# Attention and gated FFN on one core: a tile's scores are made one slot ahead of the slot in which VectorE takes them

## What is computed

```
Q, K, V = x @ W.T + b           # 16 heads of 16
scores = Q @ K.T / 4            # 512 x 512 per head
thresh = 31st largest of a row
scores = where(scores < thresh, -inf, scores)
context = softmax(scores) @ V
x = layernorm(x + context @ Wo.T + bo)
h = silu(x @ wg.T) * (x @ wu.T)
x = layernorm(x + h @ wd.T)
```

## Time and profile before

| | |
|---|---|
| median of 3 runs | 3061.3 us (3058.01 to 3065.76) |
| the profiled execution | 3046.8 us |
| its span | 3045.0 us |
| its mean granted TensorE clock | 0.951 |
| instructions | 81353 |

### The profile page before, as it was taken

One profiled execution on the slowest core, in us unless ns is written; L12 is line 12 of the kernel. 1 busy time (PEld: TensorE's weight loads), 2 busy tenths in 40 slices (PEclk: granted clock), 3 DMA queues, 4 the chain that ended last, 5 costly groups with the idle time before them and its releaser, 6 DMA issues.

```text
span 3045.0 us, 81353 instructions
## 1 busy us (share of the span) xinstructions
PE 2680.3 (88%) x21045; PEld 1454.1 (48%) x21375; DVE 2481.3 (81%) x12298; ACT 2480.9 (81%) x5894; POOL 2407.2 (79%) x1677
## 2 busy tenths in 40 slices
PE   5889989989998988889989999988989898899985
PEld 2444544545454444444545454444545454454443
DVE  4888888888888878888888888878888888888831
ACT  3788889888888977798888889978879887888931
POOL 1787988888888877788888889877869887888861
PEclk7889999999999999999999999999999999999976
DMA  2211111020111101011020111102011110202000
GB/s 81 48 25 38 28 39 39 25 47 26 41 25 40 39 22 43 18 41 39 25 46 25 43 23 44 36 25 46 26 36 30 34 43 19 47 20 50 2 15 7
DMA packets 91147, 102.67 MB, mean 34 GB/s; under 512 B 34514, under 2 KB 52947, under 8 KB 90579
## 3 DMA queue, kind: packets, MB, share of 16 engines
q1 hardware_dynamic: 88544, 93.73, 12.9%
q10 hardware_dynamic: 2034, 2.76, 0.3%
HBM read 20.86 MB, written 8.39 MB: 10 GB/s over the span
## 4 chain that ended last, share of the span: by engine, by line
PE 36%; DVE 19%; issue 14%; SPq 11%; POOL 10%; ACT 6%; DMA 2%; DVEq 1%; ACTq 0%; POOLq 0%
POOL mask L1070 8%; DVE cand L843 7%; PE bench L679 6%; SPq L349 6%; SPq L348 5%; PE Y_ps L608 5%; PE bench L673 4%; PE ST_ps L623 3%; DVE S L836 3%; PE Y_ps L606 3%; PE ctxT_ps L637 3%; PE bench L549 3%; PE ST_ps L620 2%; PE Y_ps L605 2%; ACT above L467 2%
## 5 line engine op out<-in xcount | busy, mean ns | idle before, releaser
L1070 POOL TENSOR_SCALAR mask<-S,thr,mb 128x512 bf16<-128x512 f32 x1024 | 2119.6, 2083 | 44.1 <-POOL mb L1064 30.0
L843 DVE MAX8 cand<-Y_ps 128x8 f32<-128x128 f32 x4096 | 1072.5, 282 | 5.3 <-issue 5.3
L457 ACT ACTIVATE junk<-S,at_zero,slope 128x512 bf16<-128x512 f32 x1024 | 824.6, 805 | 89.6 <-DVE S L836 89.5
L836 DVE TENSOR_SCALAR_CACHE_REDUCE S<-S_ps,na 128x512 f32<-128x512 f32 x1024 | 756.0, 738 | 163.2 <-PE S_ps L595 145.8
L467 ACT ACTIVATE above<-S,s,steep 128x512 bf16<-128x512 f32 x1024 | 824.5, 805 | 0.6
L475 ACT ACTIVATE PT<-ST_ps 128x512 f32<-128x512 f32 x1024 | 596.7, 583 | 205.7 <-PE ST_ps L623 200.2
L595 PE MATMUL S_ps<-KS,QS 64*128 64x512 f32 x1024 | 520.3, 508 | 4.2 <-DVE S L836 3.6
L608 PE MATMUL Y_ps<-KS,QS 64*128 64x512 f32 x1024 | 520.2, 508 | 0.0
L606 PE MATMUL Y_ps<-above,nbig 128*128 128x512 bf16 x1024 | 398.3, 389 | 85.4 <-DVE cand L843 57.4
L620 PE MATMUL ST_ps<-QS,KS 64*128 64x512 f32 x1024 | 415.4, 406 | 6.2 <-POOL mask L1070 6.2
L623 PEld LDWEIGHTS ST_ps<-nbig,mask 128*128 128x128 bf16 x4096 | 236.7, 99 | 382.5 <-issue 382.5
(11 more groups left out here) (125 smaller groups left out, 3682.1 us busy)
## 6 DMA issues: line engine op xcount, KB each, us to landing
QS<-Qhi SPq DMA_DIRECT2D x512, 32.0 KB, 2.0
KS<-Khi SPq DMA_DIRECT2D x512, 32.0 KB, 2.0
KS<-Klo SPq DMA_DIRECT2D x512, 32.0 KB, 2.0
QS<-Qlo SPq DMA_DIRECT2D x512, 32.0 KB, 2.0
xTs<-in_xT SPq DMA_DIRECT2D x17, 512.0 KB, 3.7
xs<-in_x SPq DMA_DIRECT2D x16, 512.0 KB, 3.9
out<-xs SPq DMA_DIRECT2D x16, 512.0 KB, 3.0
hT<-in_wgT ACTq DMA_DIRECT2D x1, 768.0 KB
```

The lines of the kernel that those rows point to most:

```text
L457: nc.scalar.activation(junk[:, :], S[:, score_place(j)[0], :], ACT.Tanh, bias=at_zero[:, :], scale=slope[:, hb, col:col + 1], accum_out=s0 ...
L836: nc.vector.tensor_scalar(S[:, at, :], S_ps[n % 2][:, :], na[:, hb, col:col + 1], None, ALU.add, op1=ALU.max, accum_out=rmax[:, n % RING:n ...
L843: mx = nc.vector.max(cand[:, j % CANDS, i, :], Y_ps[j % 2][:, i * BW:(i + 1) * BW])
L1070: nc.gpsimd.tensor_scalar(mask[:, h % MASKS, t, :], S[:, score_place(j)[0], :], thr[:, r:r + 1], mb[:, r:r + 1], ALU.is_lt, op1=ALU.add).t ...
```

## The change

TensorE's slot n now makes the scores of tile n+1 instead of those of tile n. Tile 0's scores are made ahead of slot 0 of batch 0, and slot 63 of a batch makes those of tile 0 of the next batch, except in the last batch, which for this reason stands outside the loop. The loop on TensorE therefore runs over batches 1 to 14, seven per turn. `scores` itself is unchanged but for a blank line (all later lines move by one): called for tile T+1 it waits until tile T-1 is evacuated. The other engines' programs are unchanged.

```
-TURN_OF, ACT_TURN_OF = 5, 7
+TURN_OF, ACT_TURN_OF, PE_TURN_OF = 5, 7, 7
...
-            def slots(b, first, rest):
+            def slots(b, first, rest, last=False):
                 for n in range(TILES):
                     T = b * TILES + n
                     if due(BELOW, n, first, rest):
                         below(T, n, first)
-                    if not rest:
-                        scores(T, n, b, first)
+                    if not rest and n + 1 < TILES:
+                        scores(T + 1, n + 1, b, first)
+                    if not rest and n + 1 == TILES and not last:
+                        scores(T + 1, 0, b + 1, False)
                     if due(TURNED, n, first, rest):
                         turned(T, n, first)
...
+            scores(0, 0, 0, True)
             slots(0, True, False)
...
-            with pe.Fori(1, B, TURN_OF) as b:
-                for i in range(TURN_OF):
+            with pe.Fori(1, B - 1, PE_TURN_OF) as b:
+                for i in range(PE_TURN_OF):
                     slots(b + i, False, False)
+            slots(B - 1, False, False, True)
             slots(B, False, True)
```

## The result

The changed kernel takes 3119.75 us (median of 4 runs, 3111.07 to 3124.09) against 3061.69 us before (4 runs); the ratio is 1.019 (95% interval 1.017 to 1.021), that is 52 to 63 us slower. Forecast were 3106 us and +45. The profiled execution of after has a span of 3122.3 us. It lies high among its runs and that of before low, so the two profiles differ by 77 us where the medians differ by 58.

What follows compares the result with a forecast made beforehand. No engine leads: TensorE is busiest and takes turns with VectorE. Waits and steps sum to 3.0 us a batch, +45 us over 15 batches on the 3061.3 us median: 3106 us, range 3076 to 3131 (8 in 10: 3050 to 3145).

Steps and rivals of the forecast that it cites:

- Slot 59: Scores wait for late evacuation 58, with TensorE's full down stretch right behind: +1.8 us a batch, bounds 0 and 1.8.
- slot 63: Turned scores 0.33 us later, VectorE's evacuation 0.46 us earlier: nothing, bounds -0.5 and +0.3 us.
- slots 0 to 10: Waits of 0.1 us each, 0.33 us in slots 3 and 7: nothing if TensorE's idle time stays, 1 us if not.
- 31 to 41: Steps in slots 35 and 39, with TensorE waiting around the transposes of 38 and 39: nothing, up to 0.6 us.
- Slot 11: VectorE's normalisation delays evacuation 10, so scores wait with the query projection behind them: +0.6 us, bounds 0.3 and 0.6.
- Slots 42 to 56: Three steps of 0.33 us in slots 43, 47, 51, less 0.43 us idle time: +0.6 us, bounds 0.2 and 1.0.
- The step: In 16 slots a batch (n mod 4 = 3) scores share a half with the below product and queue: 0.33 us each.
- Slots 14 to 31: Steps and late evacuations covered by SyncE's stacking copies and the load of xT: nothing, up to 1.3 us.
- The gains: VectorE's waits only move; a full stretch returns at most one evacuation, 0.75 us, at its end; none counted beyond slot 63.
- the lead pays: Rival: VectorE and ScalarE one evacuation ahead at ends of full stretches: -2.3 us a batch, 3027 us, chance 0.12.
- The loop: TensorE's body of seven batches instead of five, last batch behind it, one jump back instead of two: nothing.
- The marks named beforehand: Signs in the new profile: VectorE's score wait gone, TensorE's evacuation wait 30 us or more; wrong if maxima waits below 100.

Runs made afterwards that it cites:

- Experiments 2: Kernel before, no lead, scores in their own slot but waiting for the evacuation of tile T-1: ratio 1.019 to the kernel before, +58 us.
- 5: Changed kernel, but scores of tiles 59 and 60 made in their own slots: ratio 1.005 to the kernel before, +14 us.
- 6: Kernel before with the lead for tile 60 alone, its scores made in slot 59: ratio 1.016 to the kernel before, +50 us.
- experiment 10: Changed kernel with three filler copies of product L621 before the scores in slot 59, batches 1 to 15: ratio 1.014 to the kernel before, +43 us.
- experiment 7: Kernel before with the first turned product (L620) issued twice in slots with n mod 4 = 3: ratio 1.002 to the kernel before, +7 us.
- experiment 12: Changed kernel with the lead for tiles 0 to 8 only, other tiles in their own slot: ratio 1.0015 to the kernel before, +5 us.
- experiment 1: Kernel before with the loop part alone, seven batches per turn and batch 15 behind the loop, no lead: ratio 0.999 to the kernel before.
- experiment 4: Changed kernel with VectorE evacuating right behind the block maxima, ahead of bench work and moments: ratio 1.004 to the kernel before, +13 us.
- experiment 3: Kernel before with the score product issued twice in slots with n mod 4 = 3: ratio 1.001 to the kernel before.

## Why the prediction was right, step by step

**Slot 59 was the largest term, and is.** Forecast +1.8 us for the wait. Measured: 4.07 us before in 13 of 14 batches (5.29 in one, with a clock of 0.75), 5.77 us where the clock held, so +1.70. The assumed 0.15 us from the evacuation to the scores was 0.06. Experiments 2, 5 and 6 show that the cause is this wait, and above all in this place: the wait in every slot, without the lead, gives the whole loss (+58), the wait in slot 59 alone +50, and the change without it wins 44 of 58 us back.

**The step that failed is what stands behind it.** In 9 of 14 batches the slot took 7.35 to 7.44 us, 1.65 us on top, and in one 9.04, because the clock fell to half behind the idle time. The average is +2.9 instead of +1.8, 16 us in 15 batches, and experiment 10 wins 15 us by shortening the idle time from 1.20 to 0.50 us and not the wait. The length of the idle time alone does not decide it: before the change TensorE was idle 1.1 to 1.4 us ahead of the same slot in every batch (1.38 in the earlier trace rows), and the clock fell in one of 14; in the change the idle 1.20 us is the same in the four batches in which the clock held. What tips it is open.

**How near the number came is in part luck.** Forecast were 3.0 us a batch, the traces show 4.5. Slot 59 has 1.1 of the missing 1.5. The other errors below run from -1.0 to +1.2 us and only happen to leave 0.4 or 0.5. Against the medians 13 us are missing, against the two profiles 32.

**A slip in the range.** Its lower end takes 0.5 us for slot 59, where the walk through the batch gives 0, and leaves out slot 63 (-0.5); its upper end leaves out the bounds of slots 0 to 10 (1.0), 31 to 41 (0.6) and 63 (0.3). From the walk's own bounds it would have been wider, 3061 to 3160.

**Slot 11**, forecast +0.6: +0.55, and +0.13 in slot 13. Right to 0.1 us.

**Slots 42 to 56**, forecast +0.6: +0.3 up to slot 54. The step was mis-sized. In slot 51 and 52 of the change, batch 8:

```profile
1641.40 0.49 PE L609 MATMUL Y_ps<-KS,QS 64*128 64x512 f32 x1
1641.74 0.39 PE L596 MATMUL S_ps<-KS,QS 64*128 64x512 f32 x1
1641.97 0.39 PE L621 MATMUL ST_ps<-QS,KS 64*128 64x512 f32 x1
...
1644.06 0.50 PE L609 MATMUL Y_ps<-KS,QS 64*128 64x512 f32 x1
1644.07 0.49 PE L596 MATMUL S_ps<-KS,QS 64*128 64x512 f32 x1
1644.40 0.39 PE L621 MATMUL ST_ps<-QS,KS 64*128 64x512 f32 x1
```

In the slot with the shared half the scores do start 0.34 us behind, but the third product only 0.23 us behind them, so L621 comes 0.57 us after L609 where a normal slot has 0.34: the step is 0.23. Slots 51, 55 and 63 grow by 0.20 to 0.23. The Trainium skill's figure for a product of 512 columns, about 216 ns ("TensorE: Matmul & The Clock Gate", Back-to-back issue gap), was the better one here, and the row that I preferred shows the step behind the first product of a half; the one behind it is shorter. By experiment 7 all these steps together cost 7 us of the 58.

The cover was misread too. The 0.43 us of idle time that the forecast took off is not there: it is five gaps of 0.07 to 0.16 us at places where the trace of before lacks the record of L605. What covers instead does not show as idle time. In slot 43 of batch 8, before and after:

```profile
1586.22 0.40 PE L623 MATMUL ST_ps<-nbig,mask 128*128 128x128 bf16 x4
1586.59 1.20 PE L673 MATMUL bench<-x1T,wu 128*128 128x512 f32 x4
...
1620.41 0.40 PE L624 MATMUL ST_ps<-nbig,mask 128*128 128x128 bf16 x4
1620.61 1.18 PE L674 MATMUL bench<-x1T,wu 128*128 128x512 f32 x4
```

The bench product started 0.37 us behind the first mask product before and 0.20 behind it after. So 0.17 of the step of 0.23 us goes into a slack ahead of the bench product; it is so in slots 43 and 47 of every batch, which grow by 0.04 to 0.06 us. Slot 51 has no such slack and pays 0.21.

**Slots 14 to 31**, forecast nothing: +0.9 us. The load of xT, which was to cover, ends the wait of the projection only 3 times instead of 9. Slots 16 and 21 add 0.2 and 0.3. Slots 24 and 25 add 1.4, of which 23 and 26 give 0.9 back: the scores start 1.94 us late (2.0 forecast), and with the clock at half behind them (L621 of slot 24 takes 0.62 us in batch 8) the cover is not enough. The bound of 1.3 us held.

**The gains.** Slots 0 to 8 did win 1.0 us and 55 to 58 0.6 us, more than I allowed. But ScalarE was last behind the first: in slot 9 of batch 8 TensorE waits until ScalarE has copied the flags out of the bench (L446), which a ScalarE without a gap delivers no earlier. The copy of the context (L490) was done 0.63 us before the product started; behind it stood an exponentiation and then the flags.

```profile
1526.90 0.66 PE L647 MATMUL bench<-ident,ctxr 128*128 128x128 f32 x4 [1.27 <-ACT flag_i L446]
```

```profile
1524.87 0.83 ACT L457 ACTIVATE junk<-S,at_zero,slope 128x512 bf16<-128x512 f32 x1
...
1525.67 0.60 ACT L490 ACTIVATE ctxr<-ctxT_ps 128x512 f32<-128x512 f32 x1
1526.14 0.60 ACT L475 ACTIVATE PT<-ST_ps 128x512 f32<-128x512 f32 x1
1526.62 0.15 ACT L446 ACTIVATE flag_i<-bench 1x9 int32<-1x9 f32 x1
```

Over the span TensorE's product of slot 9 (L647) waits 16 times for this copy, 18.0 us in all; before the change it was six times and 1.9 us. In experiment 12 it is 16 times and 18.4 us.

That ScalarE and not VectorE is what ends last there is the point from which the rival "the lead pays" would have decided, and experiment 12 shows it alone. The win before slot 59 is lost in slot 59.

**The loop**: nothing, as forecast (experiment 1).

**The marks named beforehand**: VectorE's wait for scores gone, and TensorE's wait for evacuations above 30 us: seen. Slots 59 and 24 have 33 of the 38 us of it in batches 1 to 14, slot 11 under 1. In each slot with n mod 4 = 3 the scores start 0.33 us or more behind the below product: seen. TensorE's busy time can't be judged, for the missing records. TensorE's wait for maxima fell from 163 to 59 us, which I had called a sign of being wrong. It was not one, since the kernel got slower all the same: of the 104 us, 52 came back as waits for evacuations and 16 as waits for the flags in slot 9. The rest I put down to TensorE working longer, at the lower clock or on the added steps, which no run shows.

No version beat the kernel before. The one I would try next is experiment 4 with the lead taken out where it only adds the step; it was not run.

## What to carry to other kernels

Moving a producer one slot ahead with the same two buffers also moves its wait on the consumer one slot nearer, and everything queued behind it inherits that wait: before such a change, list for each slot when the consumer ends against when the producer starts, and look for the one slot in which lateness meets a full stretch. If the lead stays, the consumer should take the buffer first thing in its slot; that order wins 44 us with the lead and costs 153 us without it. And a product that is nearly free beside a partner on the other half of the array is not free one place further on: tile parity decides the partner.

## What the runs showed of the hardware

Behind a wait of 1.7 us, 1.2 us of it idle, the granted clock of slot 59 was 0.77 instead of 1.00 in 9 of 14 batches and 0.62 in one, and in experiment 6 a product of 0.39 us then took 0.63. The same delay with 0.50 us idle kept the clock in 11 of 14 (experiment 10). Yet 1.4 us of idle time a few products earlier, before the change, cost the clock in one batch of 14. Half of a wait's price can lie behind it. Of three products in a row on the same half, the second starts 0.34 us behind the first and the third 0.23 us behind the second; a product on the other half starts within 0.01 us of its partner, and 256 of them more cost nothing that can be measured (experiment 3, ratio 1.001).
